# Where the projections' input tiles live and when they are loaded, in a planned attention and FFN kernel on one core

## The reference

```python
# attention: 16 heads of two 32-wide maps, 4 key/value heads
q, k, v = x @ Wq, x @ Wk, x @ Wv
q1, q2, k1, k2 = rope(halves of q and k)
a1 = softmax(q1 @ k1.T * scale + causal_mask)
a2 = softmax(q2 @ k2.T * scale + causal_mask)
out = (a1 - lam * a2) @ v
out = group_norm(out) * gn_w + gn_b, times (1 - LAMBDA_INIT)
x = layernorm(x + out @ Wo)
# FFN: ternary weights, E = 2048
hidden = silu(x @ ternary(W_up).T) * (x @ ternary(W_gate).T)
x = layernorm(x + hidden @ ternary(W_down).T)
```

## Time and profile before

| | |
|---|---|
| median of 3 runs | 2219.04 us (2218.55 to 2219.58) |
| the profiled execution | 2216.09 us |
| its span | 2214.3 us |
| busy: PE, DVE, ACT, POOL | 97%, 77%, 65%, 54% of the span |
| mean granted TensorE clock | 0.992 of full |

### The profile page before, as it was taken

How to read it: one execution, slowest core, us unless ns; L and a number is a source line. 1 busy time by engine, 2 the same in 40 slices (tenths; PEclk the granted TensorE clock), 3 DMA queues, 4 the chain that set the end, 5 groups by cost and what they waited for, 6 DMA issues and landing times.

```text
span 2214.3 us, 41402 instructions
## 1 busy us (share of the span) xinstructions
PE 2141.2 (97%) x13442; PEld 1380.0 (62%) x13442; DVE 1702.5 (77%) x3829; ACT 1431.8 (65%) x3322; POOL 1187.0 (54%) x1919
## 2 busy tenths in 40 slices
PE   8999999899999999999999999999999999999998
PEld 4666667566666666666766666666666666644443
DVE  4888887889889888888778888878888888733333
ACT  0667777677687777767667767767677777622232
POOL 0676666677665555555545555655554555431232
PEclk9999999999999999999999999999999999999999
DMA  7666665867761213223632323342432112021000
GB/s 263 198 213 186 200 189 186 262 187 213 219 176 61 70 49 106 82 69 114 186 92 70 93 63 89 99 129 65 142 96 77 53 49 84 24 71 53 1 20 20
DMA packets 257428, 255.49 MB, mean 115 GB/s; under 512 B 31296, under 2 KB 199360, under 8 KB 255168
## 3 DMA queue, kind: packets, MB, share of 16 engines
q1 hardware_dynamic: 246016, 220.26, 33.2%
q10 hardware_dynamic: 11200, 32.58, 4.6%
HBM read 181.48 MB, written 71.30 MB: 114 GB/s over the span
## 4 chain that ended last, share of the span: by engine, by line
PE 79%; DVE 8%; issue 4%; POOL 4%; ACT 3%; DMA 1%; ACTq 0%; DVEq 0%; SPq 0%; POOLq 0%
PE PS L1154 19%; PE PS L1077 10%; PE PS L1096 10%; PE PS L1141 10%; PE PS L1163 9%; PE PS L1058 9%; PE PS L1120 8%; DVE e_long L1421 2%; PE PS L1127 2%; POOL linv L1346 1%; DVE e_long L1492 1%; ACT dt_long L1205 1%; PE PS L1062 1%; ACT e_long L1215 1%; POOL coef L1347 1%
## 5 line engine op out<-in xcount | busy, mean ns | idle before, releaser
L1215 ACT ACTIVATE e_long<-e_long,nmax 128x768 f32<-128x768 f32 (+3 forms) x512 | 505.9, 989 | 207.2 <-DVE nmax L1421 201.2
L1346 POOL TENSOR_TENSOR linv<-lsum,powers 128x2 f32<-128x2 f32 x512 | 405.4, 792 | 420.4 <-ACT e_long L1215 336.5
L1421 DVE CUSTOM_DVE_ANT_0 e_long<-PS,mask_b 128x768 f32<-128x768 f32 (+3 forms) x512 | 517.3, 1020 | 73.6 <-PE PS L1077 56.1
L1077 PE MATMUL PS<-kstk,qstk 128*128 128x384 f32 (+5 forms) x1536 | 465.7, 410 | 23.3 <-DVE nmax L1421 10.9
L1077 PEld LDWEIGHTS PS<-kstk,qstk 128*128 128x128 f32 x1536 | 268.6, 190 | 157.3 <-issue 92.7
L1492 DVE SCALAR_TENSOR_TENSOR e_long<-e_long,coef 128x1024 f32<-128x1024 f32 (+3 forms) x256 | 276.9, 1082 | 67.0 <-POOL coef L1347 66.6
L1205 ACT ACTIVATE dt_long<-PS 128x512 f32<-128x512 f32 (+3 forms) x544 | 258.5, 514 | 103.9 <-PE PS L1058 99.3
L1215 ACT ACTIVATE e_short<-e_short,nmax 128x384 f32<-128x384 f32 (+3 forms) x512 | 283.8, 559 | 17.1 <-DVE nmax L1421 16.1
L1359 POOL TENSOR_TENSOR hid<-th,hid 128x512 f16<-128x512 f32 x128 | 148.0, 1159 | 255.4 <-ACT hid L1257 132.8
L1120 PE MATMUL PS<-xT,wr 128*128 128x512 f32 x560 | 267.7, 606 | 13.8 <-DMA wr<-in_w_proj 8.7
L1058 PE MATMUL PS<-ident,e_long 128*128 128x128 f32 x1664 | 239.7, 275 | 11.9 <-DVE e_long L1492 8.7
(11 more groups left out here) (125 smaller groups left out, 3275.2 us busy)
## 6 DMA issues: line engine op xcount, KB each, us to landing
qstk<-dq SPq DMA_DIRECT2D x512, 128.0 KB, 2.9
dq<-hl SPq DMA_DIRECT2D x25, 1024.0 KB, 5.5
wr<-in_w_proj ACTq DMA_DIRECT2D x48, 512.0 KB, 4.5
kstk<-dk SPq DMA_DIRECT2D x64, 256.0 KB, 5.2
da<-ra SPq DMA_DIRECT2D x32, 512.0 KB, 3.3
at_sb<-da SPq DMA_DIRECT2D x32, 512.0 KB, 4.1
wt<-in_w_up SPq DMA_DIRECT2D x16, 512.0 KB, 5.7
wt<-in_w_gate SPq DMA_DIRECT2D x16, 512.0 KB, 6.1
```

Source lines behind the costliest of these rows:

```text
L1077: last = nc.tensor.matmul(slot[:, h, :], qstk[:, duo % 4, 2 * r + m, :].bitcast(F32R), kstk[:, g % 2, m, h * w:(h + 1) * w].bitcast(F32R), ...
L1215: nc.scalar.activation(e, e, ACT.Exp, bias=nmax[:, u % 8:u % 8 + 1], scale=-1.0, accum_out=lsum[:, n % 4, m:m + 1]).then_inc(s_exp, 1)
L1346: link(nc.gpsimd.tensor_tensor(linv[:, a % 8, :], lsum[:, a % 4, :], mone, ALU.pow))
L1421: nc.vector.tensor_tensor_reduce(out, slot, mask, -1.0, -NEG, ALU.add, ALU.min, nmax[:, u % 8:u % 8 + 1]).then_inc(s_negmax, 1)
```

## The change

The table of homes is written anew. For batch elements 0, 1 and 2 a pass uses either homes 0 to 3 of `xT` or all four homes of `x_second` (now numbered 6 to 9), by turns: passes 5 and 7 use `x_second`, passes 6 and 8 use `xT`. All four parts of these passes therefore wait for the pass before the last. Passes 9 and 10 (element 3) rotate through the six homes of `xT`: pass 9 has homes 4, 5, 0, 1, pass 10 has 2, 3, 4, 5. `x_front` looks the previous user up. The first load of `at_sb` waits for the last job of pass 7 (`X_LAST`) and no longer for that of pass 3. In the planner's table the loads of x and w are counted as landing after 8 us instead of 6.5, and the store of a rotated unit after 8 instead of 6. No arithmetic changes, and the number of loads and their sizes stay.

```diff
--- before.py
+++ after.py
@@ -99,7 +99,6 @@
 
 ROT_DOUBLE = 14
 
-
 X_HOMES = 6
 PREP = 24
 
@@ -162,19 +161,25 @@
 
 
 ONCE = len(PASSES) - 2 * (B - 1)
-LAST_ONCE = [max(p for p in range(ONCE) if PASSES[p][1] == h) for h in range(2)]
+
+X_LAST = max(p for p, (b, h, _) in enumerate(PASSES) if b < B - 1 and (h == 0) != (b == 0))
 
 
 def x_home(p, c):
 
-    at = 4 * (p - ONCE + 1) + c if p >= ONCE else c
-    return at % X_HOMES, at // X_HOMES
+
+    b, h, _ = PASSES[p]
+    if b < B - 1:
+        return (c, b) if (h == 0) == (b == 0) else (X_HOMES + c, b)
+    home = (4 * h + c + 4) % X_HOMES
+    return home, B - 1 if home < 4 else h
 
 
 def x_front(p, c):
 
-    at = 4 * (p - ONCE + 1) + c - X_HOMES
-    return None if at < 0 else LAST_ONCE[0] if at < 4 else ONCE - 1 + at // 4
+    home, _ = x_home(p, c)
+    users = [q for q in range(p) if any(x_home(q, k)[0] == home for k in range(DC))]
+    return users[-1] if users else None
 
 
 def x_load(p, c):
@@ -207,8 +212,8 @@
 TERN_AT = [100 + int(3 * i) for i in range(PREP)]
 
 HAND_OVER = {"pe": .3, "act": .4, "dve": .3, "pool": .3}
-LANDS = {"load q": 4.5, "load k": 7.5, "load v": 6.0, "store v": 7.0, "store rotated": 6.0, "store a": 4.5, "load a": 6.5,
-         "store out": 2.5, "load wo": 9.0, "load x1": 8.0, "load weight": 12.0, "load x": 6.5, "load w": 6.5, "load rope": 5.0, "load lambda": 6.0, "load first": 2.5}
+LANDS = {"load q": 4.5, "load k": 7.5, "load v": 6.0, "store v": 7.0, "store rotated": 8, "store a": 4.5, "load a": 6.5,
+         "store out": 2.5, "load wo": 9.0, "load x1": 8.0, "load weight": 12.0, "load x": 8, "load w": 8, "load rope": 5.0, "load lambda": 6.0, "load first": 2.5}
 
 
 def width(n):
@@ -416,7 +421,7 @@
     elif what == "store a":
         out = [ITEM("settle", a)]
     elif what == "load a":
-        out = [ITEM("store a", 8 * (a // 8) + 7), ITEM("fill", P_LAST[LAST_ONCE[1]], 1)]
+        out = [ITEM("store a", 8 * (a // 8) + 7), ITEM("fill", P_LAST[X_LAST], 1)]
         if a >= 2:
             out.append(ITEM("fill", JOB("wo", (a - 2) // 8, 0, (a - 2) % 8, 0), 3))
     elif what == "load wo":
@@ -777,8 +782,7 @@
         F = [PS[:, m, :] for m in range(BANKS)]
 
 
-        s_xin = [sem(f"s_xin{k}") for k in range(X_HOMES)]
-        s_xsecond = [sem(f"s_xsecond{k}") for k in range(DC)]
+        s_xin = [sem(f"s_xin{k}") for k in range(X_HOMES + DC)]
         s_win = [sem(f"s_win{k}") for k in range(2)]
         s_qin = [sem(f"s_qin{k}") for k in range(4)]
         s_kin = [sem(f"s_kin{k}") for k in range(2)]
@@ -907,6 +911,9 @@
         def t4_of(u):
             return x1[:, 4:8, :] if rotated_home(u) else t4
 
+        def x_at(home):
+            return xT[:, home, :] if home < X_HOMES else x_second[:, home - X_HOMES, :]
+
         def v_home(i):
 
             return th[:, i + 1, :].rearrange("p (t d) -> p t d", t=2) if i in (1, 2) else vst[:, :, :]
@@ -963,7 +970,7 @@
             def load_a(i):
                 b, k = divmod(i, NT)
                 if i == 0:
-                    sp.wait_ge(s_ffull, INDEX[P_LAST[LAST_ONCE[1]]] + 1)
+                    sp.wait_ge(s_ffull, INDEX[P_LAST[X_LAST]] + 1)
                 if k == 0:
                     for slot in range(2):
                         sp.wait_ge(s_rast[slot], 16 * 4 * (b + 1))
@@ -1013,12 +1020,10 @@
             for what, a, b in ORDER["sp"]:
                 if what == "load first":
                     src = x_parts[b, :, a * BANK:(a + 1) * BANK]
-                    if a == 0:
-                        sp.dma_start(xT[:, b, :], src).then_inc(s_xin[b], 16)
-                    else:
-                        if b == 0:
-                            sp.wait_ge(s_xin[1], 16)
-                        sp.dma_start(x_second[:, b, :], src).then_inc(s_xsecond[b], 16)
+                    home = X_HOMES * a + b
+                    if home == X_HOMES:
+                        sp.wait_ge(s_xin[1], 16)
+                    sp.dma_start(x_at(home), src).then_inc(s_xin[home], 16)
                 elif what == "store v":
                     store_v(a)
                 elif what == "store rotated":
@@ -1099,13 +1104,9 @@
 
             def x_part(job, c):
 
-                p = pass_of(job)
-                if p < ONCE and PASSES[p][1]:
-                    pe.wait_ge(s_xsecond[c], 16)
-                    return x_second[:, c, :]
-                home, load = x_home(p, c)
+                home, load = x_home(pass_of(job), c)
                 pe.wait_ge(s_xin[home], 16 * (load + 1))
-                return xT[:, home, :]
+                return x_at(home)
 
             def fill(job, piece):
                 bank = F[BANK_OF[job][0]]
@@ -1222,7 +1223,7 @@
                 if front is not None:
                     act.wait_ge(s_ffull, INDEX[P_LAST[front]] + 1)
                 at = T * b + BANK * h
-                act.dma_start(xT[:, home, :], x_parts[c, :, at:at + BANK]).then_inc(s_xin[home], 16)
+                act.dma_start(x_at(home), x_parts[c, :, at:at + BANK]).then_inc(s_xin[home], 16)
 
             def load_w(i):
                 if i >= 2:
```

## The result

The changed kernel takes 2236.43 us in the median of 4 runs (2235.08 to 2238.38), 1.0074 times the kernel before (95% interval 1.0058 to 1.009). It is slower by 17 us, where 10 us less was forecast. The kernel before, timed beside it, took 2219.31 us in the median of 4 runs. The profiled execution of the changed kernel took 2236.56 us.

The account below looks back on a forecast made before the run. PE bounds the kernel, busy 2141.2 of 2214.3 us. The 10 us gain, other terms inside it or 0, gave 2216.1 - 10 = 2206.1 us profiled, 2209.0 as median with 2.95 added; range 2198 to 2225.

Parts of the forecast that it names:

- The gaps at the pass boundaries: Before passes 5 to 8 V can follow at once; at most 11.1 us idle and 6.9 us of clock go.
- rival 1: Gaps go, but spare time comes back elsewhere in the same stretch: gain 0 to 4 us, 2215 to 2219; chance 0.20.
- The gain up to step 128: Passes 5 to 8, before mixing: between 8.8 and 18.0 us saved, taken as 10, near the rotation chain's figure.
- O's late start: Unit k, first behind V: O starts 5.45 to 9.31 us after E instead of 1.2; the 27.7 us excess goes.
- Everything behind PE's spare time is conserved work: A fill done in a gap between passes need not be done after step 128, where PE is full.
- sign of failure: The prediction fails if passes 5 to 8 take as long as before from first fill to last.
- The table's later landings: Passes 1 to 3: raised figures change only the order, not loads; cost 0, bounds -2 and +2 us.
- The order laid anew: All lists after the first microsecond change; one late fill inside a pass more or less is +7 or -7 us.
- rival 3: Reordering behind 549 us adds a late `y` or `wo` start, 2 to 7 us per place: 2219 to 2226; chance 0.12.
- Rival 2: Unit k's early E and O hold banks, PE stands 6.9 us per boundary: 2222 with three, 2229 with four; chance 0.13.
- The wait on `at_sb`: Its first load waits for pass 7's last job, ended at 443.0, but is issued at 584.35: margin 141 us, cost 0.
- The loads themselves: 24 x loads move earlier, zero in sum; unit k's weight load behind them may land late: 0 to 3.3 us, taken 0.5.

Follow-up runs that it names:

- homes_only: The changed kernel with the table of landings as before (store 6.0, x and w 6.5), so only the homes are new: 2228.35 us (1.004).
- before_rot8: The kernel before with one number changed, the store of a rotated unit counted at 8 us instead of 6.0: 2252.66 us (1.015).
- homes_old_order: The new homes with every engine's list in the kernel before's order, except pass 5's first two x loads, issued later: 2214.44 us (0.998 of the kernel before).
- homes_old_spread: New homes in the old order, with ACT issuing the x loads of passes 5 to 8 mid-pass, behind a weight load: 2213.74 us (0.9976 of the kernel before).

## Why the prediction was wrong

- **The gaps at the pass boundaries.** Right that they go: V follows within 1.3 us at three of the four ends and within 2.9 at the last. Wrong that their idle time goes with them: from pass 4's last fill to step 128 PE's idle time fell from 27.6 to 22.7 us, where the four gaps had held 11.1. The rest came back elsewhere, which is rival 1.
- **The gain up to step 128, put at 10 us by way of the chain.** The sum came out near, by luck: lost time fell from 49.9 to 38.2 us, which is 11.7. But 2.9 of it is the wait for the first matmul, 6.8 is the clock and only 2.0 is other idle time. The working behind the 10 us failed at two steps. O's late start should have gone, and E and O of k should have stood 1 to 3 us apart; they stand 3.3 to 10 us apart, and 18.7 of the 27.7 us of excess stay. And I had turned a chain that is further ahead into idle time saved. In homes_only the chain is 24.3 us ahead, and lost time to step 128 is 43.2 against 41.2: the attention fell back instead.
- **"Everything behind PE's spare time is conserved work."** True, and it cuts the other way too. After step 128 only projections can fill PE until the first `wo`. The new order had pass 8 stretched over that place and pass 9 behind it, 19.3 us more were lost there, and 5.5 more between steps 176 and 496. Passes 5 to 8 took 421.3 us from first to last fill instead of 402.4, which the prediction had named as its sign of failure, and the leftover stretch before the last `wo` grew from 59 to 77 us.
- **The table's later landings, put at 0 with bounds of -2 and +2.** This and the next are the steps that failed most. I asked what the machine waits for longer, and the answer, nothing, was right. The figures act through the order alone. In this change they are 8.1 of the 17 us (2236.4 against homes_only's 2228.4), and the new order with the homes alone is the other 9, where a gain of 10 was forecast. In the kernel before one of them by itself costs 33 us (before_rot8).
- **The order laid anew.** I had the term, rival 3, with 2 to 7 us and a chance of 0.12. Its size is what the disturbed kernels show: +3.8, +8.2, +14.7 and +27.5 us for neutral changes of the kernel before, and 13.9 us between homes_old_order and homes_only. It was the largest term of the case, and for the order of the kernel before all four draws lie on the slow side. The forecast and its range should have started from there.
- **Rival 2** had the right picture, a filled bank that waits for `t4` with nothing else to do, and the wrong place: not unit k at the boundaries, but q2 and q3 at the end of pass 8, 10 and 5 us of idle time and clock. Whether the held banks are what costs there is not shown.
- **The wait on `at_sb`.** Right: pass 7 ended at 438.9, the first load was issued at 555.8, and `wo` began at 567.4, 24 us earlier than before.
- **The loads themselves.** Right: the trace of the changed kernel puts no wait of PE down to `wr` but the one at the start.
- **The two loads at the start.** Missed. The kernel before had the row, 8.65 us of PE waiting for `wr`; I counted the 24 x loads and let all four of pass 5 move from 130.9, where the first two of them had been issued at 0.73, and did not ask what stands behind those. They let PE start 3.3 us earlier and are worth 1.5 to 3 us.

What stays open: what in the order of the kernel before makes it better than its neighbours by 4 to 28 us, where the homes save their 2 us, whether filling the gaps is worth anything in an order that is otherwise kept (no kernel here has that), and the 5.2 us that are not lost time.

## What to carry to other kernels

Where a planner lays the instructions of all engines, an edit has two prices: what it does in the present order, and what a new order costs; the second is found by disturbing the table by a hundredth or a tenth of a us, and was 4 to 28 us here. Try the edit in the old order first: the homes in the old order, with the loads off the boundaries, gave 2213.7 us, and with new orders anything from 2214.6 to 2255.2 us. A chain that is further ahead is no time saved until a window shows less idle time.

## What was not expected of the hardware

Two x loads of 256 KB ahead of the first weights made those land 6.9 us after issue (issued at 1.65) instead of 4.5 (issued at 0.73). PE started at 8.65 and 5.34 us. Both loads were issued by ACT, beside four of SP. The Trainium skill, page "DMA: Bandwidth & Descriptors", section "Issuing engines are not separate DMA queues", says that transfers of all issuers run on the same 16 engines and interleave. The two landings don't speak against it, and don't test it for different issuers either, since the loads that moved have the same issuer as the weights.

Five loads issued in a row by ACT take 2.3 us of its stream at the end of pass 5. PE, which waits for ACT's copy, waits 0.92 us instead of 2.05 there when four of them stand elsewhere (homes_old_spread against homes_old_order).
